# Attention row sums: VectorE's 32x32 transposition from PSUM instead of two-column matmuls

## The reference

```python
q = ch @ W_q_comp.T
k, v = jnp.split(ch @ W_kv_comp.T, 2, axis=-1)      # 64 columns each, one head
scores = jnp.einsum('btd,bsd->bts', rope(q), rope(k)) * scale
attn = jax.nn.softmax(jnp.where(causal, scores, -1e30), axis=-1)
o = jnp.einsum('bts,bsd->btd', attn, v)
z = o @ W_comp2lat.T
out = z @ W_to_kv + z @ W_out_res.T + b_out_res
```

## Time and profile before

| | before |
|---|---|
| time, median of 3 runs | 1816.95 us (1816.46 to 1821.04) |
| time of the profiled execution | 1810.25 us |
| its span | 1808.4 us |
| PE busy in the span | 1729.9 us (96%) |
| DVE busy in the span | 1169.6 us (65%) |
| ACT busy in the span | 751.4 us (42%) |
| attention part, start to end of the span | 1484 to 1808.4 us |

### The profile page before, as it was taken

The page is one execution under the profiler, slowest core; times in us unless marked ns, Lnnn a source line. Parts: engine busy times, 40 slices in busy tenths (PEclk is TensorE's granted clock), DMA queues, the critical chain, the costliest instruction groups (busy, mean ns, idle before and its releaser), DMA issues. The chain is left out here.

```text
span 1808.4 us, 27930 instructions
## 1 busy us (share of the span) xinstructions
PE 1729.9 (96%) x8349; PEld 1379.7 (76%) x8349; DVE 1169.6 (65%) x2284; ACT 751.4 (42%) x1296; POOL 664.0 (37%) x676
## 2 busy tenths in 40 slices
PE   5699999999999998999999999999999989999998
PEld 3588787787777786788778877778888867777776
DVE  7777677777777663455555555555555537878787
ACT  3232332233223322333333333333333348878885
POOL 2544554445454442333433433433433421111110
PEclk9799999999999999999999999999999999999999
DMA  7767777756777655644544546555444429799896
GB/s 251 247 197 229 244 224 216 254 194 194 209 230 228 209 180 189 206 136 155 181 174 165 175 164 200 181 179 178 159 167 168 175 52 186 196 250 217 213 254 168
DMA packets 149933, 352.50 MB, mean 195 GB/s; under 512 B 20476, under 2 KB 41916, under 8 KB 149824
## 3 DMA queue, kind: packets, MB, share of 16 engines
q1 hardware_dynamic: 97276, 234.52, 39.1%
q0 software_dynamic: 43968, 104.91, 22.6%
q10 hardware_dynamic: 8580, 11.64, 2.3%
HBM read 208.24 MB, written 146.70 MB: 196 GB/s over the span
## 5 line engine op out<-in xcount | busy, mean ns | idle before, releaser
L1488 POOL DMA_INDIRECT expert_rows<-res,ids_all x143 | 149.8, 1048 | 446.3 <-ACT res L1309 437.3
L1429 DVE TENSOR_REDUCE mx<-emb 128x1 f32<-128x512 f32 (+3 forms) x288 | 175.0, 641 | 107.3 <-PE emb L1228 85.9
L70 PE MATMUL egu<-w,rT_0h 128*128 x576 | 186.4, 405 | 0.8 <-DVE rT_0l L1400 0.8
L70 PE MATMUL egu<-w,rT_1h 128*128 x568 | 182.7, 403 | 0.0
L1406 DVE TENSOR_TENSOR eh<-egu,esg 128x256 f32<-128x256 f32 x143 | 60.6, 424 | 182.9 <-ACT esg L1299 182.9
L1035 POOL DMA_INDIRECT token_list<-tok,slot x128 | 126.6, 989 | 116.6 <-DVE slot L741 80.7
L1686 ACT ACTIVATE ex<-sc 128x1024 f32<-128x1024 f32 (+4 forms) x176 | 144.3, 821 | 60.1 <-PE sc L1631 42.7
L1483 POOL DMA_INDIRECT rows<-xn_scratch,rows_all x137 | 132.6, 968 | 48.7 <-issue 43.1
L1299 ACT ACTIVATE esg<-egu 128x256 f32<-128x256 f32 x143 | 55.0, 384 | 202.9 <-PE egu L70 200.2
L1758 POOL DMA_DIRECT2D base<-expert_rows x32 | 41.8, 1538 | 252.2 <-DMA base<-base_scratch 231.4
L1630 PE MATMUL sc<-qh,khl 128*128 128x512 f32 (+3 forms) x288 | 113.1, 393 | 14.4 <-ACT pr_1h L1686 4.5
(11 more groups left out here) (283 smaller groups left out, 4506.1 us busy)
## 6 DMA issues: line engine op xcount, KB each, us to landing
w<-expert_parts SPq DMA_DIRECT2D x64, 768.0 KB, 7.8
base<-expert_rows POOLq DMA_DIRECT2D x32, 1024.0 KB, 12.8
expert_parts<-ew_h SPq DMA_DIRECT2D x32, 768.0 KB, 7.3
expert_parts<-ew_l SPq DMA_DIRECT2D x32, 768.0 KB, 8.5
x<-x SPq DMA_DIRECT2D x16, 1024.0 KB, 6.2
xn_scratch<-xn SPq DMA_DIRECT2D x16, 1024.0 KB, 8.3
base_scratch<-xb SPq DMA_DIRECT2D x16, 1024.0 KB, 11.7
base<-base_scratch SPq DMA_DIRECT2D x16, 1024.0 KB, 11.3
```

Source lines behind the costliest of these rows:

```text
L70: mm = pe.matmul(dst, w, m, start=(first and i == 0), stop=(last and i == len(terms) - 1))
L1429: dve.tensor_reduce(mx[n % 2][:, j, c:c + 1], mb[g % 2][:, 0:width], AX.X, ALU.max).then_inc(m_red, 1)
L1488: pool.indirect_dma_start(parts_d[:, :], bass.IndirectOffsetOnAxis(ap=ids_all[:, t:t + 1], axis=0), res[t % 2][:, :], None, bounds_check=2 ...
```

## The change

The two-column products and their operand `last` go. Instead, right after `output_low` of a group, DVE turns rows 32 to 63 of `ob` by four instructions, one for each block a of 32 query rows: each reads 32 partitions by 4 x 32 columns in PSUM (the a-th 32 columns of each of the four blocks of 128 queries), turns each 32x32 square and writes partitions 32a to 32a+31 of the new SBUF tile `sums`. Row 32 is the first of the rows read, so column 0 of each turned square holds the sums. The reciprocal reads those 4 columns. The gate on the `ob` bank becomes `l_turned`, counted up by the last of the four. The two small DVE instructions that made `last` go as well, and PE's first wait of the part (`ready`) hangs on the memset ahead of them.

```diff
@@ PE: outputs, project
                 if i == first[k]:
-                    after(pe, o_ev, k - 1)
-                    after(pe, l_ev, k - 1)
+                    after(pe, l_turned, k - 1)
...
                 if j == 0:
                     pe.wait_ge(o_ev, k + 1)
-                    for i in range(GT):
-                        mm = pe.matmul(ob[k % 2][:, 2 * i:2 * i + 2], oT[k % 2][1][:, i * P:(i + 1) * P], last[:, :], start=True, stop=True)
-                    mm.then_inc(l_done, 1)
@@ DVE: output_low
                 dve.tensor_tensor(rest[C:P, :], ob[k % 2][0:C, :], value(high[0:C, :]), ALU.subtract).then_inc(o_ev, 1)
 
+                by_block = ob[k % 2][ONE:ONE + 32, :].rearrange("p (j a i) -> p j a i", a=4, i=32)
+                for a in range(4):
+                    i = dve.transpose(sums[32 * a:32 * a + 32, :, :], by_block[:, :, a, :])
+                i.then_inc(l_turned, 1)
+
@@ DVE: combine
                 if j == 0:
-                    dve.wait_ge(l_done, k + 1)
-                    dve.reciprocal(lr[k % 2][:, :], ob[k % 2][:, 0:2 * GT]).then_inc(l_ev, 1)
+                    dve.wait_ge(l_turned, k + 1)
+                    dve.reciprocal(lr[k % 2][:, :], sums[:, :, 0]).then_inc(l_ev, 1)
@@ DVE: start of the part
-            dve.memset(value(qlm[2][C:P, :]), 0.0)
-            for i in range(2):
-                one = dve.tensor_tensor(last[:, i:i + 1], ident[:, ONE:ONE + 1], ident[:, C + ONE:C + ONE + 1], ALU.add)
-            one.then_inc(ready, 1)
+            dve.memset(value(qlm[2][C:P, :]), 0.0).then_inc(ready, 1)
```

More of the change, by code:

```diff
@@ L1520, in attend @@
         identb, future = masks
-        last = sb("last", [P, 2], F32R)
         ex = [sb(f"ex_{i}", [P, 2 * GROUP]) for i in range(NE)]
@@ L1526, in attend @@
         oT = [[placed(f"oT_{i}{c}", [P, GROUP], F32R, 8 * EH + (2 * i + a) * GROUP) for a, c in enumerate("hl")] for i in range(2)]
-        lr = [sb(f"lr_{i}", [P, 2 * GT]) for i in range(2)]
+        sums = sb("sums", [P, GT, 32])
+        lr = [sb(f"lr_{i}", [P, GT]) for i in range(2)]
         sc = [ps(f"sc{i}", 2) for i in range(2)]
@@ L1537, in attend @@
         o_hi, o_ev = sem("o_hi"), sem("o_ev")
-        l_done, l_ev, p_done, p_ev = sem("al_done"), sem("l_ev"), sem("p_done"), sem("p_ev")
+        l_turned, l_ev, p_done, p_ev = sem("l_turned"), sem("l_ev"), sem("p_done"), sem("p_ev")
         base_g = base_d.rearrange("(g j p) d -> g p j d", j=GT, p=P)
@@ L1732, in combine @@
                 dve.wait_ge(p_done, GT * k + j + 1)
-                dve.scalar_tensor_tensor(out=row, in0=pj[j % 2][:, :], scalar=lr[k % 2][:, 2 * j:2 * j + 1], in1=row,
+                dve.scalar_tensor_tensor(out=row, in0=pj[j % 2][:, :], scalar=lr[k % 2][:, j:j + 1], in1=row,
                                          op0=ALU.mult, op1=ALU.add).then_inc(p_ev, 1)
-            dve.memset(value(qlm[2][C:P, :]), 0.0)
-            for i in range(2):
-                one = dve.tensor_tensor(last[:, i:i + 1], ident[:, ONE:ONE + 1], ident[:, C + ONE:C + ONE + 1], ALU.add)
-            one.then_inc(ready, 1)
+            dve.memset(value(qlm[2][C:P, :]), 0.0).then_inc(ready, 1)
             for i in range(TAIL):
```

## The result

The changed kernel took 1825.6 us (median of 13 runs, 1822.4 to 1829.9) against 1817.4 us for the kernel before (13 runs beside it, 1813.1 to 1824.1): a ratio of 1.0040, 95% interval 1.0029 to 1.0051. It is 0.4% slower, 8.2 us, where I had forecast 4.8 us as the likeliest.

What follows compares the result with a forecast made beforehand. PE was taken to set the pace mostly, with a loop through DVE and two `ex` buffers binding behind some groups. -0.24 + 4.96 + 2.0 - 2.1 + 0.2 = +4.8 us on 1816.95 gave 1821.8 us, range 1812 to 1828.

Steps and rivals of the forecast that it cites:

- What bounds the kernel: Attention part: PE sets the pace mostly; behind some groups the loop through DVE's remainder and two `ex` buffers does.
- The 8.0 us of waits: Sign: ACT's waits for DVE's `pr_..l` buffers, 8.0 us in two rows shown, would grow.
- PE's 0.45 us per group: At each group's projection, removing the products takes 0.45 us from PE's program, 7.2 us in 16 groups.
- The start, -0.24 us: At the start, PE's first matmul no longer waits for two small DVE instructions: -0.24 us, for certain.
- The price of a transposition: On DVE after `output_low`: 0.286 us long, 0.31 to the next start, 1.24 us per group; bounds 0.8 and 1.8.
- In full, 4 groups: Groups 6, 11, 12, 13: DVE's added 1.24 us delays the exponentials by as much, +4.96 us.
- In part, 4 groups: Groups 2, 4, 7, 14: delay comes after 0.4 to 0.9 us slack or PE's 0.45 lead; +0.5 each, +2.0 us.
- Hidden, 7 groups: Groups 0, 1, 3, 5, 8, 9, 10: transpositions hidden, PE's gain returns up to 0.45 us; -0.3 each, -2.1 us.
- The end, +0.2 us: Group 15, with no other work covering it: the first addition starts near 1802.4 instead of 1802.21, +0.2 us.
- B: Rival: each transposition takes 0.45 us, 1.8 per group; +10 us, 1827 us. Chance 0.15.
- C: Rival: DVE's idle time hides the transpositions in all groups but the last; 7.1 us gained, 1809.9 us. Chance 0.13.
- D: Rival: products lie where PE would have waited anyway, DVE's delays likewise; no effect, 1817 us. Chance 0.05.

Runs made afterwards that it cites:

- The stand-ins: The changed kernel with each transposition replaced by a VectorE addition of 32 partitions x 140 elements, SBUF to SBUF: ratio 1.0034 to the kernel before.
- the spreading: The changed kernel with one transposition in each of four successive steps instead of four in one place: ratio 1.0017 to the kernel before.
- the copies: The changed kernel with 5 of the 24 copies given back from DVE to ACT: ratio 1.0032 to the kernel before.
- both halves: Against the kernel before: products removed with no transpositions added, ratio 0.9965; products kept with the four transpositions per group added, ratio 1.0057.

## Why the prediction was right, and where a term was off

The mechanism was right and the sum too small: +4.8 us forecast, +8.2 measured. The terms below are compared by the first profile of each kernel, with its 8.4 us.

- **What bounds the kernel.** Right. PE leads, and behind some `output_low` the loop through the two `ex` buffers does. The 8.0 us of waits from the earlier trace rows left out a third line of the same kind (3.8 us), so they grew from 11.8 and not from 8.0; that they grew stands, and most of the growth has no name in the profile. The stand-ins, the spreading and the copies each confirm it from another side.
- **PE's 0.45 us per group.** Right in size: the projection's second matmul follows the last `outputs` by 0.43 to 0.47 us less in 14 of 16 groups (0.53 in group 12, 0.42 in the last). Of 7.2 us, 4.3 to 6.4 reach the time when nothing is added, and some 2 of the rest are lost to the late rows of `base`, which the prediction didn't think of.
- **The start, -0.24 us.** PE's first matmul now follows the memset, which lasts 0.48 us, by 0.54 us instead of 0.78, so it is there.
- **The price of a transposition.** Right: 0.31 us to the next start was taken, 0.310 long and 0.33 to the next start measured, 1.31 per group and not 1.24. They don't overlap: each starts 0.01 to 0.03 us after the end of the one before. The Trainium skill, page "VectorE: DVE Perf Modes", section on two Vector instructions with no wait between them, says that an instruction which it counts as held starts only when all earlier ones have finished; these four agree with it. The 311 ns that the same page's section on the three transpose paths gives for 128x128 in bf16 is, within 1 ns, what this one takes for 32 partitions by 128 elements of 4 bytes from PSUM.
- **In full, 4 groups.** +4.96 forecast; the table has 1.25 + 1.01 + 1.05 + 1.72 = 5.0. Right in the sum of this profile, and group 13 more than its 1.24 because two steps in a row were tight. In the second profile the same four make 6.6 us, because of the clock in group 13, so that the sum came out to 0.1 us is luck.
- **In part, 4 groups.** +2.0 forecast, and 0.2 for the end, which is in the same column as group 14; 0.65 + 0.65 + 0.87 + 0.59 = 2.8 measured. 0.6 too low.
- **Hidden, 7 groups: the term that was off.** -2.1 forecast, and -0.22 + 0.14 - 0.08 + 0.55 - 0.23 + 0.30 - 0.41 = 0.05 measured. In groups 0, 8 and 10 the sorting held. In groups 1, 3, 5 and 9 PE's gain was there when nothing was added (-0.87, -0.62, -0.48, -0.86) and was lost with the transpositions. That these four are not hidden could have been read from the trace before: the exponentials of step f+3 need the first remainder behind the transpositions, and the distance between the two, less the 0.08 us that it has where nothing is to spare, is the slack. It is about 1.35 us in groups 0 and 8, but 0.85 in groups 1 and 9, 0.55 in group 5 and 0.50 in group 3, all below the 1.24 us put in. (A late start there needn't reach the chain: in group 10 this slack is nil, and the delay was still taken up.) Two steps of mine were wrong. First, I added up PE's gain of one group and the delay of the next, as if both moved the same thing. A gain moves PE alone; where the loop binds next, the later of the two counts, and PE's lead is gone. That is groups 1 and 9: PE came into group 9 with 0.6 us of lead over the kernel before (from the products and the gate of group 8), and lost it. In the changed kernel's timeline:

```profile
1694.61 1.03 ACT L1682 ACTIVATE ex<-sc 128x1024 f32<-128x1024 f32 x1 [1.81 <-DVE pr_1l L1711]
...
1695.53 1.02 ACT L1682 ACTIVATE pr_3h<-sc 128x1024 fp32r<-128x1024 f32 x1
...
1696.60 0.50 PE L1630 MATMUL sc<-qh,khl 128*128 128x512 f32 x1 [0.75 <-ACT pr_3h L1682]
```

  ACT waits 1.81 us for the first remainder behind the transpositions, its exponentials start 0.43 us later than the lag of 4.40 us that this kernel already had would put them, and PE, being early, waits 0.75 us for them, where it had no wait before the change. Second, in groups 3 and 5 I looked at the first exponentials that were late, and their own consumer had time; but ACT then ran without a pause, and the delay of the second remainder was still in the exponentials two steps on, which PE did wait for.
- **The end, +0.2 us.** The first addition stood 2.05 us after the start of the last remainder (1800.16 to 1802.21) and stands 2.25 us after it now. Right.
- **The rivals.** B (slow transpositions) fell by the row of L1722. C (DVE's idle time takes it up) fell: there are 73.5 us of it, and most of it lies elsewhere; it took a new order to use it, and then it held only in part. D fell by both halves.

The forecast for the attention part alone is 4.8 + 0.24 = 5.1 us, and 8.4 were measured. The miss of 3.4 us (before rounding) is thus 2.1 in the hidden groups, 0.6 in the partial ones with the end, 0.1 in the full ones, and 0.6 by what the clock did at the start, which no term foresaw.

## What to carry to other kernels

Moving work from the engine that is 94% busy to one that is 77% busy can lose: ask, at the place where it is put, which engine's next instruction stands behind it and how late that one may be, and follow the delay through every instruction until the engine has an idle stretch as long as the delay, not just to the first one. Against the run with nothing in its place, a piece of 1.3 us cost 12.7 us in 16 groups; cut in four, one per step, 6.7; and with five neighbouring copies moved away as well, 3.4. (Of the 12.7 us 0.9 are the clock at the start. And the run with nothing lost some 2 us to late transfers, which makes all three prices too low.) Look at what else keeps its own pace, as well: with attention faster, it was the transfers of `base` that DVE waited for. And don't add a gain on one engine to a delay on another: where they meet, the later one counts. Run the two halves of such a change apart: here one is worth 0.35% (0.18 to 0.52), and the other costs 0.57% (0.36 to 0.78).

## What I had not expected of the hardware

- PE's clock falls for some microseconds at the start of the attention part, in some executions only. Ahead of it PE sits idle for 2.4 to 2.6 us, in those where the clock stays as well as in those where it falls; what decides between them, no run here shows. In one of the two profiles of the changed kernel it also fell after 1.36 us of idling (group 13, see the table); in five other runs it stayed up after the same pause. The granted clock over the first 5 us from PE's first scores was 0.66 in the kernel before and in the changed one, and 1.00 with the stand-ins. In the changed kernel it was at half speed, the lower of the two levels (1.2 GHz), from the first matmul on, in the one before only after 1 us. The windows, of PE alone, of the kernel before, the changed one and the one with the stand-ins, each in its own fence:

```profile
1484.55:1489.55 5.00, 4.68 (x14) 0.66 0.53 73
```

```profile
1488.34:1493.34 5.00, 4.46 (x11) 0.66 0.43 72
```

```profile
1485.80:1490.80 5.00, 3.77 (x15) 1.00 0.44 69
```

  Between these cases lie 0.8 us of time at the scores of the second step (-0.16 to +0.68 against the kernel before), which is as much as some of the groups.
- A product of 128x128 weights with two columns isn't nearly free: four of them took 0.37 us of PE from start to start, 0.09 each, and 0.08 us more on the matmul behind them.
- A 32x32 transposition of 4-byte values from PSUM runs at the pace of other DVE instructions of 128 elements: 0.310 us for 32 partitions by 128, against 0.286 for the reduction over 128 elements in the earlier trace rows.
